# A graph product in units of 1 MB, with one tile in four as three short-format products

## The reference

```python
def _L1_gnn_ref(h, adj, simlar, W_proj, b_proj, W_gcn, b_gcn):
    sim = jnp.tanh(adj * simlar)                      # simlar is adj here
    filt = sim * (adj > 0).astype(sim.dtype)
    vals, idx = jax.lax.top_k(filt, T)                # T = 350
    ...
    h2 = jnp.tanh(h @ W_proj + b_proj)
    feat = jax.nn.relu(new_adj @ (h2 @ W_gcn) + b_gcn)
    return feat
x = _layernorm(x + _L0_gnn_ref(x, adj, adj, ...), axis=-1)
x = _layernorm(x + _L1_gnn_ref(x, adj, adj, ...), axis=-1)
```

## Time and profile before

| | us |
|---|---|
| median of 3 runs (1440.57 to 1447.23) | 1446.28 |
| the profiled execution | 1447.29 |
| its span, first to last instruction | 1443.4 |
| TensorE busy | 1354.4 |
| VectorE busy | 1062.1 |
| ScalarE busy | 909.9 |
| granted TensorE clock, mean | 0.971 of full |

### The profile page before, as it was taken

The page is one execution under the profiler, slowest core; times in us unless marked ns, Lnnn a source line. Parts: engine busy times, 40 slices in busy tenths (PEclk is TensorE's granted clock), DMA queues, the critical chain, the costliest instruction groups (busy, mean ns, idle before and its releaser), DMA issues. The chain is left out here.

```text
span 1443.4 us, 11276 instructions
## 1 busy us (share of the span) xinstructions
PE 1354.4 (94%) x3652; PEld 618.4 (43%) x3652; DVE 1062.1 (74%) x1312; ACT 909.9 (63%) x952; POOL 46.0 (3%) x68
## 2 busy tenths in 40 slices
PE   5999999888999999999999999999979967999996
PEld 4444444354444444444444444444434433444442
DVE  1334433357789999999999999999928868475773
ACT  2565545305568888887878788787725545465553
POOL 0000000100010000010100100100000000000000
PEclk8999999989999999999999999999989978999998
DMA  6977787215213233242332424222062108888822
GB/s 223 348 267 272 277 286 275 101 7 220 99 65 144 102 116 131 93 155 88 119 129 95 153 88 154 94 96 79 1 250 77 44 4 324 314 294 299 300 98 60
DMA packets 53823, 228.80 MB, mean 159 GB/s; under 512 B 9928, under 2 KB 15752, under 8 KB 36232
## 3 DMA queue, kind: packets, MB, share of 16 engines
q1 hardware_dynamic: 51200, 225.55, 43.9%
q10 hardware_dynamic: 2568, 2.58, 0.5%
HBM read 223.82 MB, written 4.29 MB: 158 GB/s over the span
## 5 line engine op out<-in xcount | busy, mean ns | idle before, releaser
L1119 PE MATMUL t_y_ps<-mask,x_sb 128*128 128x512 f32 x1536 | 667.6, 596 | 11.2 <-DVE mask L1046 11.2
L1119 PEld LDWEIGHTS t_y_ps<-mask,x_sb 128*128 128x128 f32 x1536 | 292.6, 191 | 379.8 <-issue 360.6
L1046 DVE TENSOR_TENSOR mask<-mask 128x1536 f32<-128x1536 f32 x256 | 449.6, 1757 | 0.0
L894 ACT ACTIVATE mask<-mask,ones 128x1536 f32<-128x1536 f32 x256 | 399.3, 1560 | 0.0
L1032 DVE TENSOR_SCALAR mask<-mask,e_cols 128x512 f32<-128x512 f32 x512 | 228.0, 487 | 22.7 <-PE t_y_ps L1119 18.7
L887 ACT ACTIVATE mask<-mask,t_minus_e 128x512 f32<-128x512 f32 x256 | 184.6, 722 | 93.2 <-PE t_y_ps L1119 91.6
L282 PE MATMUL ns_ps<-pieces,x_sb 128*128 128x512 f32 x512 | 231.6, 609 | 6.6 <-POOL pieces L150 6.6
L1686 PE MATMUL p_ff_ps<-mask,p_g_all 128*128 128x512 f32 x512 | 224.0, 598 | 9.1 <-ACT mask L1625 9.1
L167 ACT ACTIVATE signs<-pieces 128x2048 fp8e4<-128x2048 f32 x64 | 122.3, 1911 | 50.3 <-DMA pieces<-in_adj_c 28.7
L282 PEld LDWEIGHTS ns_ps<-pieces,x_sb 128*128 128x128 f32 x512 | 97.6, 194 | 130.6 <-issue 130.5
L1686 PEld LDWEIGHTS p_ff_ps<-mask,p_g_all 128*128 128x128 f32 x512 | 97.7, 192 | 129.6 <-issue 120.4
(11 more groups left out here) (178 smaller groups left out, 632.7 us busy)
## 6 DMA issues: line engine op xcount, KB each, us to landing
pieces<-in_adj_c SPq DMA_DIRECT2D x64, 1024.0 KB, 5.0
mask<-in_adj_c SPq DMA_DIRECT2D x64, 1024.0 KB, 4.9
mask<-in_adj_t SPq DMA_DIRECT2D x32, 2048.0 KB, 8.5
mask<-scratch_shifts SPq DMA_DIRECT2D x8, 1536.0 KB, 7.9
pieces<-in_x_t SPq DMA_DIRECT2D x1, 2048.0 KB, 11.5
scratch_ns_t<-ns_sb ACTq DMA_DIRECT2D x8, 256.0 KB, 5.8
p_g_x_t<-in_x_t SPq DMA_DIRECT2D x8, 256.0 KB, 2.9
p_g_ns_t<-scratch_ns_t SPq DMA_DIRECT2D x8, 256.0 KB, 3.2
```

Source lines behind the costliest of these rows:

```text
L894: nc.scalar.activation(t, t, ACT.Exp, bias=ones[:, :], scale=-1.0).then_inc(exped, 1)
L1046: nc.vector.tensor_tensor(term(n), term(n), a, ALU.mult).then_inc(terms, 1)
L1119: mm = nc.tensor.matmul(y_ps[c % 2][h][:, :], x_sb[:, k, :], term(n)[:, h, :], start=k == 0, stop=k == NB - 1)
```

## The change

The graph phase of the usual path is rewritten as split_graph_phase, fully unrolled. The operand comes in 64 units of 1 MB, of four tiles each, 128x2048, from another layout of adj that exists already (adj_c). They lie in a ring of 14 units in the same 16 MB buffer; eight are prefetched, and unit u is loaded when the products of unit u-14 are done. Of each unit the first tile is divided: hi is its copy rounded to the short format float32r, lo the rest, tile - hi, in the same format; g_hi and g_lo are the same for the blocks of g that meet these tiles. The tile's product is g_hi*hi + g_lo*hi + g_hi*lo. The other three tiles are multiplied in float32 as before. ScalarE makes hi (and g_hi), VectorE lo (and g_lo); four slots hold hi and lo. Of the eight units of a chunk ScalarE squares the last one itself. VectorE squares two units ahead. turn and add_x1 stand after the fourth unit of the next chunk. The root at the end is taken chunk by chunk on VectorE, with a seed from the exponent and three Newton rounds, in place of Sqrt and reciprocal; y is kept in x1's place.

```diff
+SPLIT = (1,)
+CUT_SLOTS = 4
+ON_ACT = NPIECE - 1
+def load_unit(engine, dram, keep, u):
+    c, g = divmod(u, NPIECE)
+    engine.dma_start(keep["flat"][:, u % G_RING * PW:(u % G_RING + 1) * PW].rearrange("p (k n) -> p k n", n=CW),
+                     dram["adj_c"][c, :, g * PIECE:(g + 1) * PIECE, :]).then_inc(keep["unit_loaded"][u % G_RING], 16)
...
+        @block.sync
+            for u in range(FIRST_UNITS, NPIECES):
+                if u >= G_RING:
+                    sp.wait_ge(products, u - G_RING + 1)
+                load_unit(sp, dram, keep, u)
...
+        @block.scalar
+            def tanh(u):
+                n = split_of(u % NPIECE)
+                if u % NPIECE == ON_ACT:
+                    act.wait_ge(loaded[u % G_RING], 16 * (u // G_RING + 1))
+                    nc.scalar.activation(unit(u), unit(u), ACT.Square).then_inc(squared_act, 1)
+                    act.wait_ge(squared_act, u // NPIECE + 1)
+                else:
+                    act.wait_ge(squared_a, u + 1 - (u + NPIECE - ON_ACT) // NPIECE)
+                nc.scalar.activation(unit(u), unit(u), ACT.Tanh).then_inc(filtered, 1)
+                act.wait_ge(filtered, u + 1)
+                if u >= CUT_SLOTS:
+                    act.wait_ge(products, u - CUT_SLOTS + 1)
+                nc.scalar.copy(hi[u % CUT_SLOTS][:, 0:n, :].rearrange("p k n -> p (k n)"), unit(u)[:, 0:n * CW]).then_inc(cut_hi, 1)
...
+            for tiles, at in cut_tiles:
+                nc.scalar.copy(g_hi[:, :, at, :], tiles).then_inc(g_hi_made, 1)
+            for u in range(NPIECES):
+                c, g = divmod(u, NPIECE)
+                tanh(u)
+                if c and g == 2:
+                    relu(c - 1)
+                if c and g == 5:
+                    square_y(c - 1)
...
+        @block.vector
+            def cut(u):
...
+                dve.wait_ge(cut_hi, u + 1)
+                a, b = (half[u % CUT_SLOTS][:, 0:n, :].rearrange("p k n -> p (k n)") for half in (hi, lo))
+                nc.vector.tensor_tensor(b, one, a, ALU.subtract).then_inc(cut_lo, 1)
+            def add_x1(c):
+                dve.wait_ge(turned, c + 1)
...
+            def finish(c):
+                dve.wait_ge(squared, CHUNK * (c + 1))
...
+                for i in range(NEWTON):
...
+            square_a(0)
+            square_a(1)
+            dve.wait_ge(g_hi_made, len(SPLIT))
+            for tiles, at in cut_tiles:
+                nc.vector.tensor_tensor(g_lo[:, :, at, :], tiles, g_hi[:, :, at, :], ALU.subtract).then_inc(g_lo_made, 1)
+            for u in range(NPIECES):
+                c, g = divmod(u, NPIECE)
+                if u + 2 < NPIECES:
+                    square_a(u + 2)
+                cut(u)
+                if c and g == 3:
+                    add_x1(c - 1)
+                if c and g == 6:
+                    finish(c - 1)
...
+        @block.tensor
+            def graph(u):
...
+                pe.wait_ge(filtered, u + 1)
+                for j in range(n, PIECE):
+                    nc.tensor.matmul(out, g_all[:, g * PIECE + j, :], one[:, j * CW:(j + 1) * CW], start=g == 0 and j == n, stop=False)
...
+                pe.wait_ge(cut_hi, u + 1)
+                for j in range(n):
+                    nc.tensor.matmul(out, w_hi[:, j, :], half[:, j, :], start=False, stop=False)
+                    nc.tensor.matmul(out, w_lo[:, j, :], half[:, j, :], start=False, stop=False)
+                pe.wait_ge(cut_lo, u + 1)
+                for j in range(n):
+                    mm = nc.tensor.matmul(out, w_hi[:, j, :], rest[:, j, :], start=False,
+                                          stop=g == NPIECE - 1 and j == n - 1)
+                mm.then_inc(products, 1)
...
+            for u in range(NPIECES):
+                c, g = divmod(u, NPIECE)
+                if g == 0 and c >= 2:
+                    pe.wait_ge(relu_done, c - 1)
+                graph(u)
+                if c and g == 3:
+                    turn(c - 1)
+            turn(NCHUNK - 1)
```

More of the change, by code:

```diff
@@ L1428, in _ @@
             sp.dma_start(b_proj[:, :], dram["b_proj"].unsqueeze(1)).then_inc(w_loaded, 16)
-            for g in range(NGRP):
-                sp.wait_ge(keep["first_loaded"][g], 16)
+            for one in keep["unit_loaded"][0:FIRST_UNITS] if "unit_loaded" in keep else keep["first_loaded"]:
+                sp.wait_ge(one, 16)
         @block.vector
@@ L1520, in prefetch_graph @@
 def prefetch_graph(engine, dram, keep):
+    if "unit_loaded" in keep:
+        for u in range(FIRST_UNITS):
+            load_unit(engine, dram, keep, u)
+        return
     for g in range(NGRP):
@@ L1698, in _, with split_of @@
             turn(NCHUNK - 1, 1)
+NEWTON = 3
+ROOT_STEPS = 3 + 3 * NEWTON
+ROOT_SEED = 1597463007.0
+G_RING = 14
+FIRST_UNITS = 8
+SPLIT = (1,)
+CUT_SLOTS = 4
+ON_ACT = NPIECE - 1
+def split_of(g):
+    return SPLIT[g % len(SPLIT)]
+def load_unit(engine, dram, keep, u):
+    c, g = divmod(u, NPIECE)
+    engine.dma_start(keep["flat"][:, u % G_RING * PW:(u % G_RING + 1) * PW].rearrange("p (k n) -> p k n", n=CW),
+                     dram["adj_c"][c, :, g * PIECE:(g + 1) * PIECE, :]).then_inc(keep["unit_loaded"][u % G_RING], 16)
@@ new lines, in split_graph_phase, with unit, rows, _ @@
+def split_graph_phase(nc, sem, dram, keep):
+    loaded = keep["unit_loaded"]
+    b_loaded, squared_a, filtered, products, cut_hi, cut_lo = (
+        sem("h_" + n) for n in ("b_loaded", "squared_a", "filtered", "products", "cut_hi", "cut_lo"))
+    squared_act = sem("h_squared_act")
+    g_hi_made, g_lo_made = sem("h_g_hi"), sem("h_g_lo")
+    relu_done, turned, y_done, centered, squared, rooted, finished, stored = (
+        sem("h_" + n) for n in ("relu_done", "turned", "y_done", "centered", "squared", "rooted", "finished", "stored"))
+    with ExitStack() as ctx:
+        m = Mem(nc, ctx, "h_")
+        b_gcn = m.sb("b_gcn", [P, 1])
+        feat_t = [m.sb(f"feat_t{b}", [P, CW]) for b in range(2)]
+        squares = m.sb("squares", [P, CHUNK, H])
+        mean, var, root, square_sums, newton = (m.sb(n, [P, NB]) for n in ("mean", "var", "root", "square_sums", "newton"))
+        hi, lo = ([m.sb(f"{n}{s}", [P, max(SPLIT), CW], F32R) for s in range(CUT_SLOTS)] for n in ("hi", "lo"))
+        g_hi, g_lo = (m.sb(n, [P, NPIECE // len(SPLIT), sum(SPLIT), H], F32R) for n in ("g_hi", "g_lo"))
+        f_ps = [m.ps(f"f_ps{b}", [P, CW]) for b in range(2)]
+        y_ps = [m.ps(f"yt_ps{b}", [P, CW]) for b in range(2)]
+        y, g_all, ident, flat = keep["y_all"], keep["g_all"], keep["ident"], keep["flat"]
+        g_tiles = g_all[:, :, :].rearrange("p (g j) f -> p g j f", j=PIECE)
+        cut_tiles = [(g_tiles[:, s::len(SPLIT), 0:n, :], slice(sum(SPLIT[0:s]), sum(SPLIT[0:s + 1]))) for s, n in enumerate(SPLIT)]
+        block = ctx.enter_context(nc.Block())
+        def unit(u):
+            return flat[:, u % G_RING * PW:(u % G_RING + 1) * PW]
+        def rows(c):
+            return slice(c * CHUNK, (c + 1) * CHUNK)
+        @block.sync
+        def _(sp):
+            sp.dma_start(b_gcn[:, :], dram["b_gcn"].unsqueeze(1)).then_inc(b_loaded, 16)
+            for u in range(FIRST_UNITS, NPIECES):
+                if u >= G_RING:
+                    sp.wait_ge(products, u - G_RING + 1)
+                load_unit(sp, dram, keep, u)
+            for c in range(NCHUNK):
+                sp.wait_ge(finished, c + 1)
+                sp.dma_start(dram["out"].rearrange("(t p) f -> p t f", p=P)[:, rows(c), :], y[:, rows(c), :]).then_inc(stored, 16)
+            sp.wait_ge(stored, 16 * NCHUNK)
+        @block.scalar
+        def _(act):
+            def tanh(u):
[11 more added lines that the diff above has]
+                nc.scalar.copy(hi[u % CUT_SLOTS][:, 0:n, :].rearrange("p k n -> p (k n)"), unit(u)[:, 0:n * CW]).then_inc(cut_hi, 1)
+            def relu(c):
+                act.wait_ge(products, NPIECE * (c + 1))
+                if c >= 2:
+                    act.wait_ge(turned, c - 1)
+                nc.scalar.activation(feat_t[c % 2][:, :], f_ps[c % 2][:, :], ACT.Relu, bias=b_gcn[:, :]).then_inc(relu_done, 1)
+            def square_y(c):
+                act.wait_ge(centered, 3 * (c + 1))
+                for q in range(CHUNK):
+                    t = CHUNK * c + q
+                    if t:
+                        act.wait_ge(squared, t)
+                    nc.scalar.activation(squares[:, q, :], y[:, t, :], ACT.Square, accum_out=square_sums[:, t:t + 1]).then_inc(squared, 1)
+            for tiles, at in cut_tiles:
+                nc.scalar.copy(g_hi[:, :, at, :], tiles).then_inc(g_hi_made, 1)
+            act.wait_ge(b_loaded, 16)
+            for u in range(NPIECES):
[5 more added lines that the diff above has]
+                    square_y(c - 1)
+            relu(NCHUNK - 1)
+            square_y(NCHUNK - 1)
+        @block.vector
+        def _(dve):
+            def square_a(u):
+                if u % NPIECE == ON_ACT:
+                    return
```

(73 more changed lines are left out.)

## The result

| | before | after |
|---|---|---|
| median, us | 1444.01 (4 runs) | 1460.28 (4 runs, 1455.92 to 1461.15) |
| profiled span, us | 1443.4 | 1458.8 |
| mean granted TensorE clock | 0.971 | 0.964 |

The changed kernel is slower: the ratio is 1.0107, with a 95% interval of 1.0072 to 1.0142. The median before is that of the three runs above and one more. The forecast was +8.7 us, the measured difference +16.3 us; 1460.3 lies in the range of 1445 to 1465.

What follows compares the result with a forecast made beforehand. TensorE, busy 94% of the page's span, was taken as the bound. Products -13.5, fill -3.8, waits +17.0, tail +1.8 gave +1.5; clock falls +7.2 made +8.7 on 1446.3: 1455.0 us, range 1445 to 1465.

Steps and rivals of the forecast that it cites:

- Products: On TensorE, one tile in four becomes three single-pass products of 0.216 us, 0.648 in place of 0.858: -13.5 us.
- Fill: At the graph phase's start, half-as-long units let products begin after 4.29 us in place of 8.13: -3.8 us.
- Load of the two other engines: Per chunk, VectorE has 25.9 us and ScalarE 22.2 plus some 3, both under TensorE's 26.2.
- The new wait: At the fifth unit's rest product, TensorE stands still 2.43 us in each of chunks 1 to 7: +17.0 us.
- R: The moment TensorE resumes after the transposes; the fifth unit's rest half was forecast for R+5.44.
- The 0.3 us that could have opened at the eighth unit: Behind finish's tiny steps, the tightest slack elsewhere: 0.3 us more per chunk, 2 us in all, could open.
- Tail: Between the last y square and the scaling, Newton's three rounds take 2.4 us, not 0.66: +1.8 us.
- Loads: Loading the operand, 8 MB per 26.2 us, and the prefetch, were to cost nothing.
- The clock: After TensorE's seven stalls, gaps of 2.27 us, each clock fall costs 1.8 us; four falls taken: +7.2 us.
- stalls without falls: Rival: TensorE's stalls bring no clock fall or one, 1447.8 to 1449.6 us; chance 0.25.
- The faster rival: VectorE's new forms run at single-source rate: 1438.2 us, or 1430.8 with the stall gone; chance together 0.09.

Runs made afterwards that it cites:

- e1: Changed kernel with VectorE's addition of x1 one unit later, after the cut of the fifth unit: 1435.2 us, ratio 0.9951 to the kernel before.
- e5: Changed kernel with TensorE doing a unit's rest product after the next unit's float32 products, except the eighth's: 1443.15 us, ratio 0.9993 to the kernel before.
- e8: Changed kernel with turn after the third unit, y squares after the fifth, ScalarE squaring a chunk's second unit instead of its eighth: 1430.1 us, ratio 0.9912.
- e3: Changed kernel without copies, cuts and short products, all tiles full float32 products: 1445.19 us, ratio 1.0006 to the kernel before.
- e6: Changed kernel with the sum over x1's rows taken twice, lengthening VectorE's chain before the fifth unit's cut: 1464.11 us, ratio 1.0146 to the kernel before.
- e2: Changed kernel with the mean summed over 16 of 128 columns, shortening VectorE's addition chain: 1444.75 us, ratio 1.0015 to the kernel before.

## Why the prediction was right, point by point

- **Products.** I took 0.216 us for a short product, from the fp8 row. It is 0.231, so a unit is 3.267 and not 3.22 us: -10.7 where -13.5 was forecast. The term was mis-sized by 2.8 us. The rule of the Trainium skill (TensorE: Matmul & The Clock Gate, Part 3, The mechanism), by which a weight load overlaps running products only where the row group differs, doesn't hold here either: loads of 0.19 us for 128x128 weights lie behind products 0.23 us apart.
- **Fill.** -3.8 forecast, -3.8 measured; one square of 2.29 us and one tanh of 1.91 us.
- **Load of the two other engines.** "Under TensorE's, but by little, so what counts is the order": e1, e5 and e8 do the same work in other orders and give 1435, 1443 and 1430 us.
- **The new wait.** The step on which all rested. With R = 1243.18 the addition started at R+0.20, the subtraction of the mean at R+1.86, the square at R+2.46 (forecast 2.47), the cut at R+4.67 (4.70), and the rest product at R+5.40 (5.44). The stall was forecast as 2.43 us and is 2.47: the wait is 2.36, and 0.11 comes behind it, since the next product starts 0.34 us later (1248.58 to 1248.92) and not 0.23. I put this down to the rest product's weight load, which had to wait too; no run changed it. e1 shows the cause of the wait. The 0.3 us that could have opened at the eighth unit did not.
- **Tail.** +1.8 forecast, +1.6 measured. Not foreseen were the 0.9 us between the last scaling and the span's end. They are there in e3 too (1436.67 to 1443.6), so they don't hang on the products; their cause wasn't tried.
- **Loads.** Nothing, as forecast: between the first and the last product no gap of TensorE waits for a DMA.
- **The clock.** Forecast: a gap of 2.27 us, "right on" the one that decides, with zero to seven falls; I took four, +7.2. Measured: a gap of 2.20 us, six falls in the profiled execution, +10.1. That the clock can fall after such a gap was right, and the price nearly so. I had set 4.54 us against 2.74; the row at full clock behind a gap reads 2.84, so the price in my own rows was 1.70, and 1.69 is what was measured. The count was a guess, and came out higher. The step that does not hold is "the gap that decides lies between 2.05 and 2.26". The four gaps of the middle phase, which no edit touches, recur with the same lengths in all nine traces of this document, and the same length turns out either way:

| gap, us | traces with a fall behind it | us for the records behind it (thirty at 2.27, else six), with a fall and without |
|---|---|---|
| 2.05 | 4 of 9 | 4.26 to 4.35; 2.84 |
| 2.27 | 5 of 9 | 14.84; 13.14 |
| 2.81 | 7 of 9 | 4.12 to 4.54; 2.84 |
| 4.88 | 9 of 9 | 4.54 to 5.47 |

Two of these rows, the first from the changed kernel's timeline, the second from that of e8; in the kernel before, both lengths went the other way:

```profile
368.39 2.84 PE L1119 MATMUL t_y_ps<-mask,x_sb 128*128 128x512 f32 x6 [2.82 <-DVE mask L1046]
```

```profile
1049.86 4.33 PE L1086 MATMUL t_es_ps<-mask,t_gat_w 128*128 128x512 f32 x6 [2.05 <-DVE mask L1020]
```

So between 2.05 and 2.8 us the length alone doesn't decide; what else has a part in it is open. Six falls of seven, and not four or five, were luck of the execution in part. The Trainium skill (same page, HAM oscillation) describes a loop that pays the clock's transition in every round, with waits of 3 to 5 us. Here shorter gaps did the same in every round of e6 (2.79 us), in six rounds of seven in the changed kernel (2.20 us), and in none of e2 (1.73 us).

Of the 7.6 us between forecast and result, 2.8 are the short format, 2.9 the two further falls and 0.9 the end of the program; the remaining 1 us is within the spread of the medians. The rivals: "stalls without falls" is e2's world, 0.5 us of VectorE's time away. The faster rival had the wrong mechanism (VectorE's forms don't run faster: 2286 ns for a square). Its 1430.8 us for a stall that is gone looks like e8's 1430.1, but the two stand on different medians of the kernel before: the rival's is 15.5 us less, e8's ratio 12.7 us less. The difference of 2.8 us is as large as the error in the price of the short products.

## What to carry to other kernels

When stages are interleaved by hand, write down for each in-order queue what stands behind every wait, and who needs it: an instruction that waits for the consumer must not stand ahead of what that same consumer needs next. Here one unit's difference in the place of a short addition decided between 1.1% slower and 0.5% faster, and with the rest of the order fitted to it 0.9% faster, though not one instruction was saved. And a stall of TensorE has two prices, its own length and, in many of the cases from about 2 us on, the lower clock after it: 2.47 + 1.69 us here. When a difference of a few microseconds is to be read from two profiles, compare the changed phase alone, since phases that no edit touched moved it by up to 4.6 us.

## What the runs showed of the hardware

A fall of the clock gets likelier as the gap gets longer, and there is no sharp bound. In the graph phase, by TensorE's rows, none of seven gaps of 1.73 us was followed by a fall, six of seven of 2.20 us, and all of seven of 2.79 us, each in one execution. In the middle phase, over nine executions, gaps of 2.05 us were in 4 of 9 and gaps of 2.81 us in 7 of 9. Half a microsecond less work on VectorE in each chunk thus saved 13.3 us, and 0.6 us more cost 6.7. A float32r product of 128x512 appears as one record. It starts 0.231 us after the last one, where one of fp8 against bf16 starts 0.216 us after, and the width of its weights doesn't matter: with 64 columns the load takes 0.14 us instead of 0.19, and the distance stays.
